# Two LayerNorm shifts on VectorE: the mean is first copied into a PSUM bank and read from there

## What is computed

```python
def _layernorm(x, g, b):
    mu = jnp.mean(x, axis=-1, keepdims=True)
    var = jnp.mean(jnp.square(x - mu), axis=-1, keepdims=True)
    return (x - mu) * jax.lax.rsqrt(var + EPS) * g + b
...
x_norm = _layernorm(x, norm_g, norm_b)                # LayerNorm 1, 256 channels
x_proj, z = split(x_norm @ in_proj_W)                 # 384 channels each
windows = _window_partition(x_proj, 2)                # 2 x 2 windows, so 4 steps
y_ssm = unpartition(0.5 * (scan_fwd + scan_bwd))      # state-space scan, 8 states, 2 directions
y_conv = gelu(depthwise3x3(x_proj) @ pw_W)
y = (alpha * y_ssm + (1 - alpha) * y_conv) * silu(z) @ out_W
x_out = x + y
h2 = _layernorm(x_out, norm2_g, norm2_b)              # LayerNorm 2
return x_out + gelu(h2 @ fuse_W1 + fuse_b1) @ fuse_W2 + fuse_b2
```

## Time and profile before

| | |
|---|---|
| median of 3 runs | 4567.81 us (4566.51 to 4570.78) |
| profiled execution | 4575.34 us |
| its span, first to last instruction | 4573.5 us |
| mean granted TensorE clock | 0.983 |
| layer 0 | up to some 2610 us of the span |
| busy in the span: PE, DVE, ACT, POOL | 4343.5, 3753.3, 3195.2, 3650.5 us |

### The profile page before, as it was taken

One profiled execution on the slowest core, in us unless ns is written; L12 is line 12 of the kernel. 1 busy time (PEld: TensorE's weight loads), 2 busy tenths in 40 slices (PEclk: granted clock), 3 DMA queues, 4 the chain that ended last, 5 costly groups with the idle time before them and its releaser, 6 DMA issues. The chain is left out here.

```text
span 4573.5 us, 78801 instructions
## 1 busy us (share of the span) xinstructions
PE 4343.5 (95%) x24000; PEld 3097.7 (68%) x24000; DVE 3753.3 (82%) x7169; ACT 3195.2 (70%) x5780; POOL 3650.5 (80%) x3475
## 2 busy tenths in 40 slices
PE   6899999999999999999999799999999999999998
PEld 3556566565656565656565588887888788878887
DVE  5898989899998999898989677777777677777775
ACT  5788887878787888788887355555555555555555
POOL 5898989898998989898989477776777677767776
PEclk8899999999999999999999899999999999999999
DMA  2011111111111111111111400031001300040000
GB/s 57 29 34 47 38 36 43 39 46 39 46 39 46 34 50 35 50 35 48 37 37 52 138 14 23 20 91 56 22 17 32 110 21 22 22 124 18 18 21 19
DMA packets 139073, 194.82 MB, mean 43 GB/s; under 512 B 18428, under 2 KB 106470, under 8 KB 138726
## 3 DMA queue, kind: packets, MB, share of 16 engines
q1 hardware_dynamic: 138728, 190.64, 13.3%
HBM read 110.90 MB, written 79.69 MB: 42 GB/s over the span
## 5 line engine op out<-in xcount | busy, mean ns | idle before, releaser
L1423 POOL TENSOR_TENSOR pl<-probs,ph 128x512 fp32r<-128x512 f32 x1024 | 1318.7, 1289 | 543.9 <-PE ps_o L1527 269.0
L828 POOL TENSOR_TENSOR dec<-dt,rates 128x384 f32<-128x384 f32 x1536 | 1493.1, 1003 | 253.9 <-ACT dt L717 198.3
L1626 ACT ACTIVATE ph<-ps_s 128x512 fp32r<-128x512 f32 x1024 | 613.3, 599 | 773.3 <-PE ps_s L1510 768.7
L1639 DVE TENSOR_REDUCE part_max<-ps_m 128x1 f32<-128x512 f32 x992 | 667.3, 688 | 343.8 <-PE ps_m L1495 343.5
L1519 PE MATMUL ps_o<-ph,values_high 128*128 128x512 f32 x2048 | 809.1, 395 | 0.1
L1519 PE MATMUL ps_o<-ph,values_low 128*128 128x512 f32 x2048 | 804.4, 393 | 0.0
L1669 DVE TENSOR_TENSOR ps_a<-probs,ps_a 128x512 f32<-128x512 f32 x992 | 682.1, 688 | 48.0 <-ACT probs L1628 40.4
L1527 PE MATMUL ps_o<-pl,values_high 128*128 128x512 f32 x2048 | 634.4, 391 | 0.0
L1628 ACT ACTIVATE probs<-ps_s 128x512 f32<-128x512 f32 x1024 | 609.5, 595 | 0.0
L986 DVE SCALAR_TENSOR_TENSOR psS<-u,bc,psS 128x384 f32<-128x384 f32 x1024 | 597.1, 615 | 1.2
L995 DVE SCALAR_TENSOR_TENSOR y_tok<-psS,bc,y_tok 128x384 f32<-128x384 f32 x960 | 554.7, 608 | 4.5
(11 more groups left out here) (184 smaller groups left out, 7458.8 us busy)
## 6 DMA issues: line engine op xcount, KB each, us to landing
values_d<-hid SPq DMA_DIRECT2D x64, 512.0 KB, 4.6
xf<-in_x_dram SPq DMA_DIRECT2D x128, 128.0 KB
xb<-in_x_dram SPq DMA_DIRECT2D x128, 128.0 KB
residual_d<-xb SPq DMA_DIRECT2D x32, 512.0 KB, 2.6
values_high<-values_d SPq DMA_DIRECT2D x32, 512.0 KB, 6.3
values_low<-values_d SPq DMA_DIRECT2D x32, 512.0 KB, 9.1
res<-residual_d SPq DMA_DIRECT2D x32, 512.0 KB, 3.3
out_dram<-res SPq DMA_DIRECT2D x128, 128.0 KB
```

Source lines behind the costliest of these rows:

```text
L828: last = nc.gpsimd.tensor_tensor(dec[:, q % RING, j - 1, :], dt[:, par, d, token_of(d, j), :], rates[:, d, n, :], ALU.mult)
L1423: nc.gpsimd.tensor_tensor(pl[:, m % DEPTH, :], probs[:, m % DEPTH, :], ph[:, m % DEPTH, :].bitcast(F32), ALU.subtract).then_inc(pl_ok, 1)
L1626: nc.scalar.activation(ph[:, m % DEPTH, :], ps_s[m % 2][:, :], ACT.Exp).then_inc(ph_ok, 1)
L1639: nc.vector.tensor_reduce(part_max[:, qt, kc:kc + 1], ps_m[r % 2][:, :], AX.X, ALU.max).then_inc(max_out, 1)
```

## The change

Both LayerNorms' `shift` step gets a second instruction. `norm_step` is given `own_bank`, the PSUM bank of the chain whose step DVE did last. It copies the 5 or 4 means from `mv` into this bank behind the state (from column 384 on), waits for the copy on a new semaphore `mean_ok`, and computes `shift` with the mean from PSUM and `std` from SBUF. The copy stands ahead of the wait for `std`. The last tile's LayerNorm 2, for which no chain is active, and LayerNorm 1 of tile 0, which is made elsewhere, stay as they were: there are 31 copies for each LayerNorm, 62 in all.

```diff
-            def norm_step(what, tile, x_in, n, stats, mv, std, shift, ok, std_ok, norm_ok):
+            means = []
+
+            def norm_step(what, tile, x_in, n, stats, mv, std, shift, ok, std_ok, norm_ok, own_bank):
...
                 else:
                     dve.wait_ge(ok, base + 2)
+                    mean = mv[:, :, 0:1]
+                    if own_bank is not None:
+                        mean = own_bank[:, INNER:INNER + n].rearrange("p (t s) -> p t s", s=1)
+                        nc.vector.tensor_copy(mean, mv[:, :, 0:1]).then_inc(mean_ok, 1)
+                        means.append(tile)
+                        dve.wait_ge(mean_ok, len(means))
                     dve.wait_ge(std_ok, tile + 1)
-                    last = nc.vector.scalar_tensor_tensor(shift[:, :, :], mv[:, :, 0:1], -1.0, std[:, :, :],
+                    last = nc.vector.scalar_tensor_tensor(shift[:, :, :], mean, -1.0, std[:, :, :],
                                                           ALU.mult, ALU.mult)
                 last.then_inc(ok, 1)
...
             def body(k, par, part):
+                own_bank = None
                 for step, tile, at in steps(DVE_ORDER, k, part):
...
                     if step.startswith("st"):
                         states(k, par, int(step[2:]) // PIECES, int(step[2:]) % PIECES)
+                        own_bank = psS[int(step[2:]) // PIECES % STATE_BANKS]
```

More of the change, by code:

```diff
@@ L349, in layer0 @@
         log1_ok, log2_ok = sem("log1_ok"), sem("log2_ok")
+        mean_ok = sem("mean_ok")
         norm1_ok, norm2_ok = sem("norm1_ok"), sem("norm2_ok")
@@ L878, in norm_step, with front @@
                     dve.wait_ge(ok, base + 2)
+                    mean = mv[:, :, 0:1]
[4 more added lines that the diff above has]
+                        dve.wait_ge(mean_ok, len(means))
                     dve.wait_ge(std_ok, tile + 1)
-                    last = nc.vector.scalar_tensor_tensor(shift[:, :, :], mv[:, :, 0:1], -1.0, std[:, :, :],
+                    last = nc.vector.scalar_tensor_tensor(shift[:, :, :], mean, -1.0, std[:, :, :],
                                                           ALU.mult, ALU.mult)
                 last.then_inc(ok, 1)
-            def front(step, f, par):
+            def front(step, f, par, own_bank):
                 if step.startswith("ln1") and f == 0:
@@ L889, in front @@
                         dve.wait_ge(x_loaded, 96 * (f + 1))
-                    norm_step(step[4:], f, xf, T + 1, stats1, mv1, std1, shift1, stats1_ok, std1_ok, norm1_ok)
+                    norm_step(step[4:], f, xf, T + 1, stats1, mv1, std1, shift1, stats1_ok, std1_ok, norm1_ok, own_bank)
                 elif step == "gd_mul":
@@ L899, in front, with back @@
                                             ALU.add).then_inc(direct_ok, 1)
-            def back(step, g, par):
+            def back(step, g, par, own_bank):
                 if step.startswith("ln2"):
@@ L904, in back @@
                         dve.wait_ge(back_dve, emptied(g, "out1")[1])
-                    norm_step(step[4:], g, xb, T, stats2, mv2, std2, shift2, stats2_ok, std2_ok, norm2_ok)
+                    norm_step(step[4:], g, xb, T, stats2, mv2, std2, shift2, stats2_ok, std2_ok, norm2_ok, own_bank)
                     return
@@ L1027, in body @@
                         states(k, par, int(step[2:]) // PIECES, int(step[2:]) % PIECES)
+                        own_bank = psS[int(step[2:]) // PIECES % STATE_BANKS]
                     elif is_back(step) or step.startswith("ln2"):
-                        back(step, tile, 1 - par)
+                        back(step, tile, 1 - par, own_bank)
                     else:
-                        front(step, tile, 1 - par if at == 1 else par)
+                        front(step, tile, 1 - par if at == 1 else par, own_bank)
                     if tile == 0 and step == "ln1_shift":
```

## The result

The changed kernel takes **4579.64 us** (median of 20 runs, 4575.12 to 4583.15), the kernel before beside it 4569.65 us (20 runs, 4566.51 to 4573.90): a ratio of 1.0021, 95% interval 1.0015 to 1.0028. It is 10 us slower; forecast were 9 us less. 4579.6 us lies outside the range of 4549 to 4571 us. The profiled execution took 4581.1 us (span 4579.3), 5.8 us more than that of before.

What follows compares the result with a forecast made beforehand. A ring of POOL and ACT was taken to bound layer 0's tiles; 28 x 0.31 = 8.7 us off the 4567.8 us median, with the count of clock falls kept at 14, gave 4559 us, range 4549 to 4571 us.

Steps and rivals of the forecast that it cites:

- The shift's wait: Layer 0's LayerNorm shift on DVE: two SBUF operands make it wait for a POOL instruction's end, 0.72 us each.
- What reaches the end of the tile: Layer 0: POOL's `acc3` comes 0.31 us earlier in each of 28 tiles, 8.7 us; DVE's further gain becomes waits.
- ACT's wait for the shift: ACT's `ln2_norm` in layer 0 waits for DVE's shift: forecast to fall from 1.96 to about 1.1 us.
- Rivals 3 and 4: Rival 3: wait only moves, 4568 to 4573 us, chance 0.10; rival 4: DVE sets the pace, 4541 us, chance 0.03.
- I keep 14: Layer 0: the count of tiles with the long `dt` wait stays 14 of 30; allowed 8 to 21, -9 to +11 us.
- The clock's term: Layer 0: where TensorE's granted clock falls, POOL waits 5.55 us for `dt` instead of 4.02, 1.53 us a tile.
- rival 2: Layer 0: the clock falls in more tiles than 14, up to 4583.5 us with all 30; chance 0.18.

Runs made afterwards that it cites:

- the unused copy: Changed kernel with the mean copied to PSUM and waited for, but the shift reading it from SBUF, plus 66 bare increments: 4567.38 us, ratio 0.9996 to before.
- the matmuls: Two unneeded 384-column matmuls in TensorE's idle stretch of each tile: on the kernel before 4551.47 us (0.9953), on the changed kernel 4547.86 us (0.9945).
- increments alone: Kernel before with 62 bare semaphore increments on DVE ahead of layer 0: 4577.16 us, ratio 1.0006.

## Why the prediction was wrong

**The shift's wait: right.** It was put down to the pair of SBUF operands and to the end of the running POOL instruction. The copy of 155 ns, the shift of 164 ns and the 0.27 us that they hold DVE are as forecast; the experiments with LayerNorm 1 alone and with the unused copy show that the pair of SBUF operands and POOL's running instruction are the cause.

**What reaches the end of the tile: right, and a little smaller.** 0.31 us a tile were forecast, 0.27 to 0.29 came (78.71 to 78.44, 77.18 to 76.89 us), and with the matmuls in both kernels 8.3 us in all against 8.7. ACT's wait for the shift fell from 1.91 (61.1 us in 32 waits) to 1.52 us (48.8 us in 32 waits) and not to 1.1: with LayerNorm 2's mean alone in PSUM it is 1.52 too (44.0 us in 29 waits), so LayerNorm 1's part adds nothing to it. That it moved ACT as well is the likely reason, and was not tested. It had no effect on the time. Rivals 3 and 4 are refuted: no wait moved to the copy, and DVE's waits for ACT grew from 188.2 to 209.6 us, which is where its saved time went.

**"I keep 14": this step failed.** The clock's term was seen and priced, 1.53 us for a tile, and the matmuls confirm the price. What was wrong is that the count was left where it was while the tile's length, which was said to move it, changed. The profile after has 22, beyond the 21 at which the range ended: +12.2 us instead of 0. This is rival 2. A long tile of 78.71 us drew at most two more behind it; with 78.44 us a run has up to nine, and with 78.47 us all the layer. The trace of before would have allowed a better weight: in its runs of three the fall comes 0.2 us earlier from tile to tile and leaves the 0.8 us in which it happens. Long tiles shorter by 0.27 us move it by 0.07 us the other way, so the runs had to get longer. Rival 2 should have had more than 0.18.

**A term that was missing.** Nothing was said of the code's place. 62 instructions more in DVE's unrolled layer 0 shift its code of layer 1; more code is loaded there (214 packets instead of 179), and DVE stalls five times. Layer 1 was 2.5 us longer in the profile after and 3.2 us in the one with increments alone. The medians of that run differ by 5.0 us, with an interval that holds no difference, and the changed kernel with the matmuls has the same 214 packets and a layer 1 of 1961.4 us. So the loads are shown, their price of some 3 us is not beyond doubt.

**What stays open.** The profiled executions differ by 5.8 us and the medians by 10; the profile of before was taken in an execution above all its 20 timed runs. With the estimate from the granted clock, 8 to 11 more long tiles are 12 to 17 us, less 8.4 us by the shorter tiles and with up to 2.5 us for layer 1: 4 to 11 us, in which the measured 10 lie. Why single tiles are 0.2 to 0.3 us longer, and where in the beat layer 0 begins, no run here sets or tells, so the count of one execution could not have been forecast; that it would probably rise could.

## What to carry to other kernels

Where an unrolled loop leaves TensorE idle for a moment in each turn, look at whether its granted clock falls behind that idle stretch in some turns and not in others. If so, a shorter turn can make the kernel slower and a longer one faster, as here, and a small saving in the turn is hard to judge by the total until the idle stretch is filled. Fill it first: here that was worth two and a half times the change. A VectorE instruction with two SBUF operands beside a busy GpSimd waited here until a GpSimd instruction ended, mostly 0.8 us, though it had 4 or 5 elements; a detour of one operand through PSUM, 0.2 us, removed the wait.

## What the runs showed that was not expected

- Adding 0.2 us of GpSimd work to each of the tiles made the kernel 7.5 us faster (ratio 0.9985), and making the change for LayerNorm 1 alone, which shortens the tiles by 0.24 us, made it 24 us slower (1.0053), both through the number of tiles with a fallen clock: 4 and 30 in the profiles, instead of 14.
- In all 181 long tiles behind the first tile the clock fell between 5.02 and 4.20 us ahead of POOL's first exponent, and whether the next tile was long too hung on how far a tile's length moved the fall: 0.20 us at 78.71 us, 0.04 us at 78.47 us.
- Two matmuls for nothing, 1.46 us in each tile, took 21 us off (0.9953).
- A two-operand SBUF instruction of 4 elements took 150 ns, 252 ns (median) or 790 ns depending only on how far the GpSimd instruction beside it had come.
- 62 instructions that do nothing, ahead of layer 0, changed the instruction loads from 179 to 214 packets and made layer 1 3.2 us longer in the profile; with 128 there were 179 to 181 packets again, and no such waits.
